# One program block for the whole decoder layer, and a new order of work in the attention's slots

## The reference

```
x = x + self_attention(layernorm(x))                     # 16 heads of 16, no mask
x = x + cross_attention(layernorm(x), ctx, ctx, mask)    # scores at masked keys := 1e-9
x = x + ffn(layernorm(x))
ffn(h) = layernorm(gelu(h @ tern(W_fc).T), w, b) @ tern(W_proj).T
tern(W) = sign(W) * min(round(|W| / (mean|W| + 1e-6)), 1)
attention(q, kv) = softmax(Q K.T / 4) V @ Wo.T + bo ;  Q, K, V = projections with bias
```

## Time and profile before

| | us |
|---|---|
| median of 3 runs | 2607.31 (2600.8 to 2608.62) |
| the profiled execution | 2609.64 |
| its span in the profile | 2607.8 |

### The profile page before, as it was taken

How to read it: one execution, slowest core, us unless ns; L and a number is a source line. 1 busy time by engine, 2 the same in 40 slices (tenths; PEclk the granted TensorE clock), 3 DMA queues, 4 the chain that set the end, 5 groups by cost and what they waited for, 6 DMA issues and landing times. The chain is left out here.

```text
span 2607.8 us, 72523 instructions
## 1 busy us (share of the span) xinstructions
PE 2210.0 (85%) x29047; PEld 1457.0 (56%) x29047; DVE 2033.7 (78%) x4023; ACT 1609.8 (62%) x2352; POOL 1026.5 (39%) x719
## 2 busy tenths in 40 slices
PE   3367888888889888888988888888865799999999
PEld 3134555555555555555555555555533477777777
DVE  5257888888888888888888888888753588888887
ACT  2245666666666666666666666665532687788776
POOL 0133443433443433344443344343221454555553
PEclk8679999999999999999999999999987899999999
DMA  3356786666677676667767666776431333333332
GB/s 86 67 88 111 125 131 119 121 127 120 123 124 125 121 119 126 118 123 129 123 122 127 118 122 124 122 126 117 82 68 36 67 83 94 97 89 81 95 97 58
DMA packets 450752, 276.75 MB, mean 106 GB/s; under 512 B 299344, under 2 KB 401104, under 8 KB 450512
## 3 DMA queue, kind: packets, MB, share of 16 engines
q1 hardware_dynamic: 447728, 270.68, 55.7%
q10 hardware_dynamic: 2784, 2.43, 0.3%
HBM read 54.87 MB, written 33.55 MB: 34 GB/s over the span
## 5 line engine op out<-in xcount | busy, mean ns | idle before, releaser
L616 ACT ACTIVATE prob<-exp_bank 128x1024 f32<-128x1024 f32 x512 | 523.0, 1022 | 289.2 <-PE exp_bank L870 285.6
L714 DVE TENSOR_REDUCE cross_mx<-score_bank 128x8 f32<-128x1024 f32 x256 | 311.0, 1215 | 136.2 <-PE score_bank L852 136.2
L714 DVE TENSOR_REDUCE self_mx<-score_bank 128x8 f32<-128x1024 f32 x256 | 310.4, 1213 | 135.1 <-PE score_bank L852 135.1
L550 POOL TENSOR_TENSOR xs<-xn,xs 128x1024 f16<-128x1024 f32 x64 | 136.1, 2127 | 686.6 <-ACT xs L643 686.6
L1267 PE MATMUL hbk<-wfcT,ffn_xhl 128*128 128x512 f16 x1024 | 265.5, 383 | 28.5 <-DMA ffn_xhl<-ffn_xs 26.6
L550 POOL TENSOR_TENSOR ahl<-attT,ahl 128x512 f16<-128x512 f32 x128 | 148.0, 1156 | 349.6 <-ACT ahl L621 349.6
L1227 DVE SCALAR_TENSOR_TENSOR ghl<-tbk,lnwc,ghl 128x512 f16<-128x512 f32 x256 | 187.9, 735 | 100.3 <-ACT ghl L1158 100.3
L1243 PE MATMUL ybk<-wpT,ghl 128*128 128x256 f16 x2048 | 260.5, 273 | 0.8 <-DVE ffn_y L1212 0.7
L1243 PEld LDWEIGHTS ybk<-wpT,ghl 128*128 128x128 f16 x2048 | 197.9, 98 | 66.0 <-DVE ghl L1227 0.9
L1158 ACT ACTIVATE ghl<-tbk,lnwc 128x512 f16<-128x512 f32 x256 | 174.0, 680 | 68.3 <-PE tbk L1257 68.3
L746 DVE STREAM_TRANSPOSE out_bank<-out_bank 128x512 f32<-128x512 f32 x256 | 183.9, 718 | 40.3 <-PE out_bank L887 40.3
(11 more groups left out here) (162 smaller groups left out, 4654.9 us busy)
## 6 DMA issues: line engine op xcount, KB each, us to landing
self_stk<-self_qk SPq DMA_DIRECT2D x768, 64.0 KB, 2.4
cross_stk<-cross_qk SPq DMA_DIRECT2D x768, 64.0 KB, 2.4
self_src<-in_x SPq DMA_DIRECT2D x32, 512.0 KB, 5.7
ctx_in<-in_ctx SPq DMA_DIRECT2D x32, 512.0 KB, 6.3
x_scratch<-xn SPq DMA_DIRECT2D x32, 512.0 KB, 5.5
ffn_src<-x_scratch SPq DMA_DIRECT2D x32, 512.0 KB, 3.8
out<-ffn_y SPq DMA_DIRECT2D x32, 512.0 KB, 3.6
self_stk<-self_negmT SPq DMA_DIRECT2D x64, 128.0 KB, 3.8
```

The costliest lines, as they stand in the source:

```text
L550: nc.gpsimd.tensor_tensor(out, src, hi, ALU.subtract).then_inc(lo_ready, 1)
L616: act.activation(prob[:, p % 3], ebank[:, :, :], ACT.Exp, scale=EXP_SCALE).then_inc(b.exp_done, 1)
L714: dve.tensor_reduce(a.mx[:, 8 * m:8 * m + 8].rearrange("p (j r) -> p r j", r=2), sbank[:, :, :].rearrange("p r (j k) -> p r j k", j=4), AX ...
```

## The change

**One block.** There is one `nc.Block`. Each engine's program is a list of pieces of the three parts; pieces of the setup stand between the first slots, each before its first use, and the FFN's first loads and body(-1) before the last two slots. All steps of the attention are written out on all engines. The setup's tables come from one set of 8 products instead of two.

```
     x2_dram = nc.dram_tensor("x2_scratch", (B, S, D), F32, kind="Internal").ap()
-    with ExitStack() as stack:
+    with ExitStack() as stack, nc.Block() as block:
         sb, _, _ = allocators(nc, stack, stack)
         sh = Shared(sb)
-        setup(nc, stack, ins, sh)
-        attention(nc, stack, ins, sh, x2_dram)
-        ffn(nc, stack, sh, x2_dram, out)
+        prep = setup(nc, stack, ins, sh)
+        att = attention(nc, stack, ins, sh, x2_dram, prep)
+        mlp = ffn(nc, stack, sh, x2_dram, out, att)
...
+        LAST = 2 * (NG + 4)
...
+        @block.sync
+        def _(sp):
+            att.load_first(sp)
+            prep.load_weights(sp)
+            att.slots(lambda s: att.sync(sp, s), 0, 3)
+            att.await_primed(sp, 1)
+            att.slots(lambda s: att.sync(sp, s), 3, 5)
+            att.await_primed(sp, 2)
+            att.slots(lambda s: att.sync(sp, s), 5, 8)
+            att.await_primed(sp, 8)
+            att.slots(lambda s: att.sync(sp, s), 8, LAST)
+            mlp.load_first(sp)
+            mlp.sync(sp, -1)
+            att.slots(lambda s: att.sync(sp, s), LAST, LAST + 2)
+            mlp.unrolled(sp, lambda i: mlp.sync(sp, i))
+            mlp.await_stores(sp)
...
+        @block.scalar
+        def _(act):
+            prep.load_small(act)
+            att.slots(att.scalar, 0, 3)
+            prep.weights_high(act)
+            att.slots(att.scalar, 3, 4)
+            prep.magnitudes(act)
+            att.slots(att.scalar, 4, 6)
+            prep.projection_out(act)
+            att.slots(att.scalar, 6, LAST)
+            mlp.scalar(-1)
+            att.slots(att.scalar, LAST, LAST + 2)
+            mlp.steps(act, mlp.scalar)
+        @block.vector
...
+            att.slots(att.vector, 0, 2)
...
+            prep.mask_parts(dve)
+            att.prime_queries(dve, 1, prep.consts)
+            prep.weights_low(dve)
+            att.slots(att.vector, 2, 4)
+            att.prime_values(dve)
+            prep.ternary(dve)
+            prep.tables(dve)
+            att.slots(att.vector, 4, 6)
...
+            prep.tables_out(dve)
+            att.prime_cross(dve)
+            att.slots(att.vector, 6, LAST)
+            mlp.vector(-1)
+            att.slots(att.vector, LAST, LAST + 2)
+            mlp.steps(dve, mlp.vector)
+        @block.tensor
...
+            prep.turn_weights(pe)
+            att.slots(att.tensor, 0, 4)
+            prep.mask_products(pe)
+            att.slots(att.tensor, 4, 6)
+            prep.turn_ternary(pe, att.maxima_out, att.exp_done)
+            prep.table_products(pe)
+            prep.await_tables(pe)
+            att.slots(att.tensor, 6, LAST + 2)
+            mlp.steps(pe, mlp.tensor)
...
-                    nc.vector.tensor_copy(lnwB[:, t], sh.lnwc[:, t:t + 1].broadcast_to([P, P]))
-                    last = nc.vector.tensor_copy(lnbB[:, t], lnb_col[:, t:t + 1].broadcast_to([P, P]))
...
-                nc.vector.tensor_copy(c2B[:, :], bank[:, 0, 0:D]).then_inc(c2_done, 1)
-                nc.vector.tensor_copy(s2B[:, :], bank[:, 0, D:2 * D]).then_inc(c2_done, 1)
...
+            for t in range(FT):
+                nc.vector.tensor_copy(lnB[:, t, 0:HALF], lnb_col[:, t:t + 1].broadcast_to([P, HALF]))
+                last = nc.vector.tensor_copy(lnB[:, t, HALF:P], sh.lnwc[:, t:t + 1].broadcast_to([P, HALF]))
...
+            pe.wait_ge(fc_out, 2)
+            for t in range(FT):
+                if t % 4 == 0:
+                    pe.wait_ge(pj_out, t // 4 + 1)
+                last = nc.tensor.matmul(bank[:, 2, 0:D], lnB[:, t], wpT32[:, t], start=(t == 0), stop=(t == FT - 1))
...
-        def step(slot, i, r):
-
-            slot(Slot(slf, crs, i, i - 3, r, r + 1))
-            slot(Slot(crs, slf, i - 2, i, r, r))
-
-        FROM, TO = 4, NG - 2
-
-        def steps(engine, slot):
-
-            for i in range(-2, FROM):
-                step(slot, i, i)
-            if engine in (nc.tensor, nc.sync):
-                for i in range(FROM, TO):
-                    step(slot, i, i)
-            else:
-                with engine.Fori(FROM, TO - 1, 2) as i:
-                    step(slot, i, 0)
-                    step(slot, i + 1, 1)
-            for i in range(TO, NG + 3):
-                step(slot, i, i)
-
+        def slots(program, first, last):
+            for n in range(first, last):
+                i = n // 2 - 2
+                program(Slot(crs, slf, i - 2, i, i, i) if n % 2 else Slot(slf, crs, i, i - 3, i, i + 1))
...
+def ffn(nc, program, sh, x2_dram, out, before):
...
+                        if s == 0 and isinstance(q, int) and q == 0:
+                            act.wait_ge(before.stored, 16 * NG)
...
+        def load_first(sp):
+            sp.wait_ge(before.stored, 16 * (NG - 1))
+            for n in range(2):
+                sp.dma_start(src[:, n], x2_groups[n]).then_inc(loaded[n], 16)
...
+        def unrolled(sp, body):
+            body(0)
+            sp.wait_ge(before.stored, 16 * NG)
+            for i in range(1, NG // 2 + 1):
+                body(i)
```

**The order in a slot, the same for both kinds.** Lines of the old and new lists, engine by engine (SP, POOL, ACT, DVE, PE):

```
-            def maxima():
-                if s.ga is not None:
...
             turn_context()
             stacks(0)
             stacks(1)
             turn_input()
+            store()
             stacks(2)
-            maxima()
-            store()
             load()
...
-            biased()
             low_outputs(b, s.gb, 0)
             deviations()
+            biased()
...
+            def maxima_rows():
+                if s.ga is not None:
+                    act.wait_ge(a.mT_out, s.ga + 1)
+                    for r in range(2):
+                        act.dma_start(a.stk[HALF * r + STACK:HALF * (r + 1), s.ra, 0].rearrange("p j k t -> p (j k) t"),
+                                      a.negmT[:, :].unsqueeze(1).broadcast_to([H, FT // 2 * KT, T])).then_inc(a.m_in, 16)
...
             split_context()
             tile(0)
+            normalise(0, 1)
             tile(1)
+            exps(0)
+            tile(2)
             split_outputs(a, s.go, 1)
-            tile(2)
-            exps(0)
+            exps(1)
             tile(3)
-            exps(1)
-            normalise(0, 1)
             exps(2)
             normalise(2, 3)
             exps(3)
+            split_norm()
             exps(4)
-            split_norm()
             exps(5)
             products_out()
+            split_outputs(b, s.gb, 0)
             exps(6)
+            values_out(0)
             exps(7)
-            values_out(0)
             values_out(1)
             maxima_in()
-            split_outputs(b, s.gb, 0)
+            maxima_rows()
             masked_weights()
...
+                    if kt == 0 and s.go is not None:
+                        dve.wait_ge(a.a_lo, 2 * s.go + 1)
+                    if kt == 1 and s.gb is not None:
+                        wait(dve, b.a_lo, 2 * s.gb)
...
             masked_values()
             outputs(a, s.go, 3)
             tile(0)
-            turn_att(a, s.go, 1)
             maximum(0)
             tile(1)
+            turn_att(a, s.go, 1)
             maximum(1)
+            tile(2)
             maximum(2)
-            tile(2)
             tile(3)
             maximum(3)
             outputs(b, s.gb, 0)
             maximum(4)
+            outputs(b, s.gb, 1)
             maximum(5)
-            outputs(b, s.gb, 1)
             turn_att(b, s.gb, 0)
             maximum(6)
             outputs(b, s.gb, 2)
...
+                if s.gb is not None:
+                    pe.wait_ge(b.exp_done, 8 * s.gb + 8)
...
             tile(0)
             tile(1)
             scores(0)
+            shifted(0)
             tile(2)
-            shifted(0)
             scores(1)
+            shifted(1)
             tile(3)
-            shifted(1)
             scores(2)
             shifted(2)
             weighted(0)
             scores(3)
             shifted(3)
             products(0, 1)
+            shifted(4)
             scores(4)
-            shifted(4)
             weighted(1)
+            shifted(5)
             scores(5)
-            shifted(5)
             products(2, 3)
+            weighted(2)
+            scores(6)
             shifted(6)
-            scores(6)
-            weighted(2)
             values(0, 1)
             scores(7)
             shifted(7)
             values(2, 3)
             turn_maxima()
+            weighted(3)
             masked_values()
-            weighted(3)
```

533 lines of the change are left out of this document (282 added, 251 removed).

## The result

The changed kernel takes **2739.99 us** (median of 4 runs, 2735.34 to 2743.38), the kernel before 2604.36 beside it: ratio 1.052 [1.050 to 1.055]. It is slower by 5.2%. I had forecast 2539.

A forecast was written before the change was run, and what follows sets the result against it. SP's DMA issues and the two heads were taken to bound the step. Terms -7 steady, -52.3 and +11.5 setup, -23.85 and +4.8 seam, -2 drain summed to -68.9: 2539 us against 2607.31, range 2480 to 2600.

The forecast's parts named there:

- What bounds the kernel: Steady step: a loop through SP's queue and two heads, summing to 57.3 us, 41 of 57 being SP's issues.
- The heads: From scores(0) to SP's next 16 stacks: PE's new order gives 5.60 and 5.71 us, saving 0.9 and 0.5 per step.
- The second queue: ACT issuing the maxima while SP issues its last stacks: +0.5 us per step, bounds nothing and 2.5.
- sign of being wrong: Steady part: SP's stacks taking over 0.8 us per issue where ACT's DMAs fall would show the forecast wrong.
- The store: In SP's queue, moved from behind the self stacks' last 8 to ahead of them: +0.66 us per step.
- POOL, ACT, DVE at nothing: These engines' new orders in each slot cost nothing, covered by the 20 us of issues in each slot.
- Sum per step: Steady part: heads, second queue and store together -0.24 us per step, -7 us over about 28 steps.
- The slower rival: Steady part: late maxima make shifted(0) hold the tiles, heads of 8.6 and 7.9 us, 2671 us in all; chance 0.08.
- The setup: Before the attention: first tile starts at 22.5 us, -52.3; work moved into slots 5 and 6 returns +11.5.
- The seam: Attention to FFN: PE's idle gap goes, -23.85 us; ACT's norm ahead of the last exponentials costs +4.8, bounds 2 and 8.
- The ends together: Setup and seam, the run's two ends, gain 62 us; a rival with half the joining gave 2569 us, chance 0.08.

The follow-up runs named there:

- e4: The changed kernel, with PE doing the products of tile(0) and tile(1) twice in every slot before it waits for the stacks; ratio 1.016 to the kernel before.
- e3: The changed kernel with SP's queue entirely as before the change, maxima and store behind stacks(2), other engines keeping their new order; ratio 1.076 to the kernel before.
- e6: The changed kernel with all five lists (SP, POOL, ACT, DVE, PE) as before the change, leaving the one block; ratio 0.982 to the kernel before, 2548.6 us.
- e5: The kernel before, with only the maxima's DMAs moved from SP to ACT, right behind the copy; ratio 1.022 to the kernel before.
- e2: The changed kernel with the store behind stacks(2) again, the maxima staying with ACT; ratio 1.040 to the kernel before.
- e1: The changed kernel with the maxima's DMAs issued by SP behind stacks(2) again, no longer by ACT; ratio 1.072 to the kernel before.
- e8: The changed kernel with tile(0) and tile(1) done twice and SP's queue entirely as before the change; ratio 1.065 to the kernel before.
- e11: The one-block kernel with the new list on PE only; SP's queue, ACT, DVE and POOL as before; ratio 1.083 to the kernel before.
- e10: The one-block kernel with new lists on ACT, DVE and POOL only; SP's queue and PE's list as before; ratio 1.077 to the kernel before.

## Why the prediction was wrong

**What bounds the kernel**: right. The loop through SP's queue and the two heads still sets the step, and SP stands first in the chain after.

**The heads**: the step that failed. Its arithmetic gave 5.60 and 5.71; the changed kernel has 7.17 (1029.72 to 1036.89) and 7.71 (1060.35 to 1068.06) in the step shown and 7.4 and 7.6 in the mean, e4 with the clock kept up 5.8 and 5.9. I took the duration of a tile, 1.40, from a trace in which the clock of the steady part is 1.00, and wrote that a faster slot is covered by "the 20 us of issues in each slot". That cover is where PE now idles. The idle piece ahead of scores(0) has two sources. With the new lists and the old queue (e3) PE idles 1.6 and 2.4 us there, against 0.2 and 1.1 with all old lists (e6); with SP's longer phases of the changed kernel it becomes 4.1 and 3.8. The Trainium skill (TensorE: Matmul & The Clock Gate, "Why this matters for your kernels") says to avoid longer idle gaps between bursts of matmuls, or the clock drops to half. The trace after agrees: 2.74 against 1.47 for the same six products. I had this rule at hand and left it out, since the trace before shows no low clock in the steady part. It was the rule that spoke against this change. Price: 3.1 us per step by e4, about 90 us in all.

**The second queue**: mis-sized. I took +0.5 per step between 0 and 2.5. The groups of 8 measured +1.3 and +1.4, 2.8 in sum, above my upper end. The prediction's own sign of being wrong, over 0.8 us per issue beside ACT's DMAs, came true with 0.92. "What lies in the queues seems to matter little" was read from a store that no other queue issued beside. The Trainium skill (DMA: Bandwidth & Descriptors, "Issuing engines are not separate DMA queues") says that the transfers of all issuing engines interleave on the same DMA engines, and that a second issuing engine saves only issue time. The runs agree with the first as far as they show it: ACT's pair makes SP's stacks issue slower (7.4 for 6.1 us) or land later (3.5 for 2.5 us in e5). What it saved in issue time, 1.24 us per pair, SP's own issues lost again.

**The store**: +0.66 forecast; +0.8 measured in the phase (22.3 less 20.1, less 1.3 for the group), and 1.3 by e2, which moves it back alone.

**POOL, ACT, DVE at nothing**: true for time on the path, and not for its consequence, the idle piece on PE. Sum per step: -0.24 forecast, +6.0 measured: +3.6 in SP's phases (forecast +1.2), +2.4 in the rest (forecast -1.4).

**The slower rival** had the right sign and the wrong mechanism: the maxima landed in time. Its mechanism is real, and e1, e3 and e8 show it where SP issues them, at more than its price (heads of 10.4 and 9.5 in e1 for 8.6 and 7.9), in part because tile(2) is slow there too.

**The setup**: the first tile starts at 24.76 (forecast 22.5, -50.0 for -52.3). The first 16 self stacks are 29.3 us earlier in the changed kernel and 36.2 in e6 (forecast -40.8). **The seam**: the gap is gone, as said. ACT, then PE, of the changed kernel:

```profile
2132.39 2.07 ACT L1288 ACTIVATE ffn_xn<-ffn_src,ffn_nmr,ffn_rstd 128x256 f32<-128x256 f32 x4 [6.49 <-DVE ffn_nmr L1338]
...
2136.64 1.02 ACT L722 ACTIVATE prob<-exp_bank 128x1024 f32<-128x1024 f32 x1 [1.09 <-PE exp_bank L988]
```

```profile
2135.14 1.03 PE L950 MATMUL exp_bank<-maskBT,pick 64*128 64x512 bf16 x4 [10.17 <-DVE ue L845]
```

The last exponentials come behind the norm, but it isn't ACT's norm that ends their wait, as the prediction had it. ACT is done with norm and copy at 2135.55; PE's products for the exponentials waited 10.17 us for DVE's `ue` (L845), which stands on DVE behind the FFN's statistics. From the last maxima's issue to the last products it was 29.6 us (1975.23 to 2004.79) and is 36.7 (2123.59 to 2160.32): +7.2 for my +4.8, inside its bounds; in e6 it is 42.7, outside. The ends together were forecast at -62. In e6's trace the first 16 self stacks start 36.2 us earlier, the last cross stacks 51.7 (at 1882.28) and the FFN's first matmul 62.9 (at 1970.95), so the ends gave 47 us: 36 for 41 in the setup, 11 for 21 in the seam.

What stays open: whether SP's stacks are held by ACT's issuing or by the bytes of its transfers, and which of the lists of ACT, DVE and POOL does the harm in e10. That the same pair costs SP's group 1.4 us in the changed kernel and 0.4 in e5 goes with where it falls, at the group's start or at its end.

## What to carry to other kernels

A reordering that lets an engine finish early can gather its idle time into one piece, and on TensorE such a piece had a price at its end here: look for what runs right after it, and whether the chain waits for that. Here 24 redundant products per step made the changed kernel 3.4% faster, though still 1.6% slower than the kernel before; the better kernel is e6, with the old lists. Lists for several engines are one design: PE's new list alone (e11), or those of ACT, DVE and POOL alone (e10), cost more than all of them. And when a transfer moves to an idle engine's queue, price what it does to the issues and the landings of the busy one.

## What the runs showed of the hardware

The clock at half its rate cost 1.3 us in the first tile after an idle piece of 3.9 us (2.74 for 1.47), and also after two pieces of 0.85 and 1.74 us in e5; after 2.1 us with 0.6 soon behind it in the kernel before, it stayed up.

Two DMAs of 128 KB that ACT issues beside SP's group of 8 make those of SP's issues longer that fall beside or right behind them (up to 1.54 us in the mean for 0.6), and where they fall on the last ones these also land later (3.5 and 3.7 us behind the start of the issue for 2.5 and 2.7).

No issue of a stack by SP took less than 585 ns, and the median of the self chain's 768 is 594, in the kernel before as after. Single ones took up to 2.0 us before and 3.3 after, and the sums of such stretches, with the transposes and the store, are what made the phases of 48 issues differ between kernels.
